# One half of the array's partitions for each head of a cross attention, and a new order of steps

## What is computed

```python
x = x + _L0_attn_ref(_layernorm(x, axis=-1), L0_attn_gamma)
x = x + _L0_xattn_ref(_layernorm(x, axis=-1), ctx_1024, ctx_1024, ...)
x = x + _L0_ffn_ref(_layernorm(x, axis=-1), ...)
```

```python
scores = jnp.einsum('bhqd,bhkd->bhqk', q, k) / jnp.sqrt(jnp.float32(dk))
scores = scores + slopes[None, :, None, None] * dist[None, None, :, :]
attn = jax.nn.softmax(scores, axis=-1)
```

## Time and profile before

| | |
|---|---|
| median of 3 runs | 316.39 us (316.10 to 316.88) |
| profiled execution, its span | 312.0 us (no other time of it is recorded) |
| busy: PE, DVE, ACT, POOL | 232.0, 177.7, 105.6, 73.2 us |
| L766 DVE reduces, x88 | 49.9 us |
| L606 ACT exponentials, x80 | 44.7 us |
| L959 PE maxima matmuls, x172 | 33.5 us |
| L980 PE score matmuls, x64 | 28.2 us |
| mean granted PE clock | 0.830 |

### The profile page before, as it was taken

How to read it: one execution, slowest core, us unless ns; L and a number is a source line. 1 busy time by engine, 2 the same in 40 slices (tenths; PEclk the granted TensorE clock), 3 DMA queues, 4 the chain that set the end, 5 groups by cost and what they waited for, 6 DMA issues and landing times.

```text
span 312.0 us, 3052 instructions
## 1 busy us (share of the span) xinstructions
PE 232.0 (74%) x993; PEld 99.4 (32%) x993; DVE 177.7 (57%) x433; ACT 105.6 (34%) x182; POOL 73.2 (23%) x122
## 2 busy tenths in 40 slices
PE   0876756587889688978998996997985599843184
PEld 0332522122323233443533344242443133223031
DVE  3148639598563678868539797672866260133160
ACT  1333332301484545245164703622611522610000
POOL 7118420001630008117100310640001080001080
PEclk9997876855959889965999998599997569995569
DMA  3790007711003400213340101436200210000221
GB/s 76 230 224 2 3 0 183 161 47 32 13 3 113 90 0 2 61 33 117 122 81 0 36 3 41 137 101 137 65 0 6 66 78 0 0 1 2 81 88 34
DMA packets 26409, 19.25 MB, mean 62 GB/s; under 512 B 12249, under 2 KB 25025, under 8 KB 26305
## 3 DMA queue, kind: packets, MB, share of 16 engines
q1 hardware_dynamic: 26393, 19.05, 23.5%
HBM read 13.64 MB, written 5.41 MB: 61 GB/s over the span
## 4 chain that ended last, share of the span: by engine, by line
PE 45%; DVE 24%; DMA 9%; ACT 8%; issue 5%; SPq 4%; POOL 3%; ACTq 0%; DVEq 0%; POOLq 0%
PE bank L1044 10%; DVE nm L766 9%; PE bank L858 5%; PE bank L1002 4%; PE bank L959 4%; SPq L306 4%; PE bank L1000 4%; PE bank L980 3%; DMA xs<-in_x_dram 3%; ACT pt L606 3%; PE bank L933 2%; DVE y L659 2%; POOL w L499 2%; PE bank L1030 2%; PE bank L901 2%
## 5 line engine op out<-in xcount | busy, mean ns | idle before, releaser
L766 DVE TENSOR_REDUCE nm<-bank 128x3 f32<-128x462 f32 x88 | 49.9, 617 | 18.2 <-PE bank L959 17.0
L606 ACT ACTIVATE pt<-bank 128x512 f32<-128x512 f32 x80 | 44.7, 597 | 26.0 <-PE bank L980 18.4
L959 PE MATMUL bank<-kA,qs 128*128 128x308 bf16 (+1 forms) x172 | 33.5, 298 | 14.1 <-DVE nm L766 7.9
L1044 PE MATMUL bank<-ym,ewT 128*128 128x512 f32 x64 | 32.4, 664 | 6.2 <-DVE ym L837 6.2
L499 POOL TENSOR_TENSOR w<-w,ab 128x512 f32<-128x512 f32 x8 | 11.9, 1506 | 99.2 <-ACT ab L530 99.2
L520 POOL TENSOR_TENSOR ym<-mask_all,y3T 128x512 f32<-128x512 bf16 x16 | 25.5, 1623 | 33.3 <-DMA mask_all<-e_scratch 33.3
L980 PE MATMUL bank<-qs,kB 128*128 128x512 bf16 x64 | 28.2, 501 | 3.4 <-ACT pt L606 2.7
L837 DVE TENSOR_TENSOR ym<-mask_all,y3T 128x512 f32<-128x512 bf16 x16 | 21.6, 1407 | 16.0 <-DMA mask_all<-e_scratch 16.0
L901 PE MATMUL bank<-y1Tg,y1T 128*128 128x512 f32 x32 | 20.8, 738 | 5.5 <-ACT w L544 3.2
L676 DVE TENSOR_REDUCE rm<-bank 128x1 f32<-128x512 f32 x16 | 11.0, 690 | 24.2 <-PE bank L902 24.2
L959 PEld LDWEIGHTS bank<-kA,qs 128*128 128x128 bf16 x172 | 12.7, 102 | 37.8 <-DVE nm L766 26.0
(11 more groups left out here) (155 smaller groups left out, 307.2 us busy)
## 6 DMA issues: line engine op xcount, KB each, us to landing
mask_all<-e_scratch SPq DMA_DIRECT2D x8, 512.0 KB, 4.7
qs<-q_scratch SPq DMA_DIRECT2D x8, 384.0 KB, 5.1
q_scratch<-qpart SPq DMA_DIRECT2D x4, 384.0 KB, 2.5
...
```

The costliest lines, as they stand in the source:

```text
L606: nc.scalar.activation(pt[:, n % PT_RING, :], ST[n % 2][:, :], ACT.Exp).then_inc(exps, 1)
L766: v.tensor_reduce(negated[:, GROUP * g:GROUP * g + heads], MX[n % 2][:, 0:heads * J].rearrange("p (s j) -> p s j", s=heads), AX.X, ALU.max ...
L959: last = mm(MX[n % 2][:, at * J:(at + heads) * J], qs[:, b % 2, a, tile(t)], kA[:, s:s + heads, a, 0:J], start=True, stop=True)
L1044: last = mm(YV[:, :], ewT[:, e, :], ym[:, e, :], start=False, stop=(e == E - 1))
```

## The change

Each head has 48 + 3 + 3 rows in one half of the partitions, 0 to 53 or 64 to 117: `place(h)` gives pair and half, heads of odd groups of four the upper one. The weights' rows are reordered on input to match (`head_rows`). There is one key stack `ks` with two buffers by batch, no zero blocks, and `kA` and `kB` go; their loads (8 + 8 of 120 KB) become 8. A part of `maxima` is three pairs for both banks: lower halves write MX[0] and upper halves MX[1], in turn, each matmul with 154 columns; both banks wait for the part before. The number and size of DVE's reduces stay. `scores` goes through the halves in turn with its two banks. The maxima are loaded into `qs` by two DMAs, not one. The orders of all engines are new; of these the diff shows the parts up to the first maxima of batch 1 or 2.

```diff
-AUG = 2 * ROWS
+AUG = ROWS
 MAXROW = AUG + 3
+USED = MAXROW + 3
+
+
+def place(h):
+    g, k = h // R, h % R
+    return g // 2 * R + k, g % 2
...
     "sync": """
-        query:0 keys:0 more_keys:0 stats1:1 mT:0 query:1 stats1:2 divide:0.0 mT:1 mask:0 query:2 divide:1.0
-        stats1:3 mT:2 mask:1 query:3 store:0 store:1 divide:2.0 mT:3 mask:2 mask:3 store:2 store:3
+        keys:0 query:0 more_keys:0 mT:0 stats1:1 query:1 mT:1 mask:0 stats1:2 query:2 stats1:3 mT:2 mask:1
+        query:3 store:0 mT:3 mask:2 mask:3 store:1 store:2 store:3
     """,
     "gpsimd": """
-        rstd1:0 sub:0 rstd1:1 weights:0 rstd2:0 sub:1 rstd1:2 rstd2:1 sub:2 rstd1:3 rstd3:0 rstd2:2 select:0
+        rstd1:0 sub:0 weights:0 rstd1:1 rstd2:0 sub:1 rstd2:1 rstd1:2 rstd1:3 sub:2 rstd3:0 rstd2:2 select:0
...
     "scalar": """
-        y1T:0 dist:0 ab:0 sub:0 self:0 weights:0 y2T:0 keys:0 query:0 y1T:1 dist:1 ab:1 sub:1 mT:0 self:1
-        scores:0.0 scores:0.1 scores:0.2 scores:0.3 scores:0.4 scores:0.5 y2T:1 query:1 y1T:2 values:0.1 dist:2
+        y1T:0 dist:0 ab:0 sub:0 self:0 weights:0 keys:0 y2T:0 query:0 y1T:1 dist:1 ab:1 sub:1 self:1 mT:0 y2T:1
+        scores:0.0 query:1 scores:0.1 scores:0.2 scores:0.3 y1T:2 scores:0.4 scores:0.5 dist:2 scores:0.6
+        values:0.1 scores:0.7 scores:0.8 scores:0.9 scores:0.10 scores:0.11 ab:2 values:0.3 aoT:0 sub:2 y3T:0
...
     "vector": """
-        stats1:0 y1:0 dist:0 rowmax:0 stats1:1 sub:0 weights:0 self:0 gather:0 y1:1 y2:0 query:0 keys:0 dist:1
-        rowmax:1 maxima:0.0 maxima:0.1 maxima:0.2 maxima:0.3 maxima:0.4 maxima:0.5 maxima:0.6 maxima:0.7
-        maxima:0.8 maxima:0.9 maxima:0.10 mcat:0 sub:1 stats1:2 self:1 y1:2 gather:1 stats1:3 y2:1 query:1
-        dist:2 maxima:1.0 maxima:1.1 rowmax:2 maxima:1.2 maxima:1.3 maxima:1.4 maxima:1.5 maxima:1.6 sub:2
+        stats1:0 y1:0 dist:0 rowmax:0 sub:0 weights:0 stats1:1 self:0 gather:0 y1:1 y2:0 keys:0 query:0 dist:1
+        rowmax:1 stats1:2 sub:1 maxima:0.0 maxima:0.1 maxima:0.2 self:1 maxima:0.3 maxima:0.4 maxima:0.5
+        maxima:0.6 maxima:0.7 maxima:0.8 maxima:0.9 maxima:0.10 mcat:0 gather:1 y2:1 y1:2 stats1:3 query:1
+        dist:2 maxima:1.0 rowmax:2 maxima:1.1 maxima:1.2 maxima:1.3 divide:0.0 maxima:1.4 sub:2 maxima:1.5
+        maxima:1.6 divide:0.1 maxima:1.7 maxima:1.8 wo:0 maxima:1.9 y3:0 self:2 maxima:1.10 mcat:1 route:0
...
     "tensor": """
-        y1T:0 dist:0 weights:0 ab:0 self:0 gather:0 keys:0 y2T:0 query:0 y1T:1 dist:1 maxima:0.0 maxima:0.1
-        maxima:0.2 maxima:0.3 maxima:0.4 maxima:0.5 maxima:0.6 maxima:0.7 maxima:0.8 maxima:0.9 maxima:0.10 ab:1
-        mT:0 self:1 gather:1 scores:0.0 scores:0.1 scores:0.2 scores:0.3 scores:0.4 scores:0.5 y2T:1 scores:0.6
-        query:1 values:0.0 y1T:2 values:0.1 dist:2 maxima:1.0 maxima:1.1 scores:0.7 divide:0.0 maxima:1.2
-        scores:0.8 ab:2 scores:0.9 maxima:1.3 maxima:1.4 maxima:1.5 scores:0.10 maxima:1.6 scores:0.11
-        values:0.2 maxima:1.7 values:0.3 divide:0.1 maxima:1.8 aoT:0 maxima:1.9 wo:0 maxima:1.10 self:2 y3T:0
-        mT:1 route:0 gather:2 mask:0 scores:1.0 scores:1.1 scores:1.2 scores:1.3 y2T:2 query:2 scores:1.4
-        experts:0 y1T:3 scores:1.5 values:1.0 scores:1.6 dist:3 maxima:2.0 values:1.1 maxima:2.1 scores:1.7
+        y1T:0 dist:0 ab:0 weights:0 self:0 gather:0 keys:0 y2T:0 query:0 y1T:1 dist:1 ab:1 self:1 maxima:0.0
+        maxima:0.1 maxima:0.2 maxima:0.3 maxima:0.4 gather:1 maxima:0.5 maxima:0.6 maxima:0.7 maxima:0.8
+        maxima:0.9 maxima:0.10 mT:0 y2T:1 scores:0.0 query:1 scores:0.1 y1T:2 scores:0.2 scores:0.3 values:0.0
+        scores:0.4 scores:0.5 dist:2 scores:0.6 maxima:1.0 values:0.1 maxima:1.1 scores:0.7 scores:0.8
+        maxima:1.2 scores:0.9 ab:2 maxima:1.3 scores:0.10 divide:0.0 scores:0.11 maxima:1.4 values:0.2
+        maxima:1.5 values:0.3 maxima:1.6 divide:0.1 maxima:1.7 aoT:0 maxima:1.8 wo:0 maxima:1.9 self:2 y3T:0
+        maxima:1.10 route:0 mT:1 gather:2 mask:0 scores:1.0 scores:1.1 y2T:2 scores:1.2 query:2 scores:1.3
+        experts:0 y1T:3 scores:1.4 values:1.0 scores:1.5 dist:3 scores:1.6 maxima:2.0 values:1.1 maxima:2.1
...
-        kA = sb("kA", [P, 2, PAIRS, JP], BF16)
-        kB = sb("kB", [P, 2, PAIRS, JP], BF16)
+        ks = sb("ks", [P, 2, PAIRS, JP], BF16)
...
-        nm = sb("nm", [P, T, H])
+        nm = sb("nm", [P, 2, T, PAIRS])
...
-        a_ps, maxed, mcat_ready, mT_ps, mT_sb = sem("a_ps"), sem("maxed"), sem("mcat_ready"), sem("mT_ps"), sem("mT_sb")
+        a_ps, maxed = [sem(f"a_ps{s}") for s in range(2)], [sem(f"maxed{s}") for s in range(2)]
+        mcat_ready, mT_ps, mT_sb = sem("mcat_ready"), sem("mT_ps"), sem("mT_sb")
...
-        GROUPS = -(-T * H // GROUP)
-        MAX_GROUPS = [range(g, min(g + 2, GROUPS)) for g in range(0, GROUPS, 2)]
+        GROUPS = -(-T * PAIRS // GROUP)
...
-            load(kA[:, :, :, :], k_aug[0], kaug_in)
-            load(kB[:, :, :, :], k_aug[1], kaug_in)
-            for par in range(2):
-                load(qs[AUG:P, par, :, :], q_aug, qaug_in)
+            for s in range(2):
+                load(ks[s * HALF + AUG:s * HALF + USED, :, :, :], k_aug[s], kaug_in)
+            for s in range(2):
+                load(qs[s * HALF + AUG:s * HALF + MAXROW, :, :, :], q_aug, qaug_in)
...
-            def stack_keys(stacks, b, s_in):
+            def stack_keys(b):
 
                 for s in range(2):
-                    load(stacks[s * ROWS:(s + 1) * ROWS, s, :, :],
-                         k_scratch[b].rearrange("(a s c) k j -> s (c k) a j", s=2, c=DK)[s], s_in)
+                    load(ks[s * HALF:s * HALF + ROWS, b % 2, :, :],
+                         k_scratch[b].rearrange("(a s c) k j -> s (c k) a j", s=2, c=DK)[s], ks_in)
 
             def stats1(b, _):
-                if b >= 1:
-                    sp.wait_ge(k_out, 3 * B * ONE)
-                    sp.wait_ge(maxed, b * GROUPS)
-                    stack_keys(kA, b, kA_in)
+                sp.wait_ge(k_out, 3 * B * ONE)
+                if b >= 2:
+                    sp.wait_ge(st_ps, (b - 1) * R * ITEMS)
+                stack_keys(b)
 
             def keys(b, _):
                 sp.wait_ge(k_ready, 1)
                 write_keys(0)
                 sp.wait_ge(k_out, 3 * ONE)
                 sp.wait_ge(kaug_in, 2 * ONE)
-                stack_keys(kA, 0, kA_in)
-                stack_keys(kB, 0, kB_in)
+                stack_keys(0)
...
-                    load(qs[s * ROWS:(s + 1) * ROWS, b % 2, :, :],
+                    load(qs[s * HALF:s * HALF + ROWS, b % 2, :, :],
                          q_scratch.rearrange("(a s c) k n -> s (c k) a n", s=2, c=DK)[s], qs_in)
-
-            def divide(b, f):
-                if f == 0 and b + 1 < B:
-                    sp.wait_ge(st_ps, (b + 1) * R * ITEMS)
-                    stack_keys(kB, b + 1, kB_in)
 
             def mT_(b, _):
                 sp.wait_ge(mT_sb, b + 1)
                 load(m_scratch.rearrange("r (a n) -> (r a) n", n=S), mT[:, :], m_out)
                 sp.wait_ge(m_out, ONE * (b + 1))
-                load(qs[MAXROW:MAXROW + 6, b % 2, :, :].rearrange("p a n -> p (a n)"), m_scratch, m_in)
+                for s in range(2):
+                    load(qs[s * HALF + MAXROW:s * HALF + USED, b % 2, :, :].rearrange("p a n -> p (a n)"),
+                         m_scratch.rearrange("(i s) w -> s i w", s=2)[s], m_in)
...
             def maxima(b, k):
-                negated = nm[:, :, :].rearrange("p t h -> p (t h)")
-                for g in MAX_GROUPS[k]:
-                    n, heads = b * GROUPS + g, min(GROUP, T * H - GROUP * g)
-                    dve.wait_ge(a_ps, n + 1)
-                    v.tensor_reduce(negated[:, GROUP * g:GROUP * g + heads],
-                                    MX[n % 2][:, 0:heads * J].rearrange("p (s j) -> p s j", s=heads),
-                                    AX.X, ALU.max, negate=True).then_inc(maxed, 1)
+                pairs = slice(GROUP * k, min(GROUP * (k + 1), T * PAIRS))
+                heads = pairs.stop - pairs.start
+                for s in range(2):
+                    dve.wait_ge(a_ps[s], b * GROUPS + k + 1)
+                    v.tensor_reduce(nm[:, s, :, :].rearrange("p t a -> p (t a)")[:, pairs],
+                                    MX[s][:, 0:heads * J].rearrange("p (s j) -> p s j", s=heads),
+                                    AX.X, ALU.max, negate=True).then_inc(maxed[s], 1)
...
             def maxima(b, k):
                 if k == 0:
-                    pe.wait_ge(kA_in, 2 * ONE * (b + 1))
+                    pe.wait_ge(ks_in, 2 * ONE * (b + 1))
                     pe.wait_ge(qs_in, 2 * ONE * (b + 1))
                     if b == 0:
                         pe.wait_ge(setup_sb, 8)
                     if b >= 1:
                         pe.wait_ge(mT_sb, b)
-                for g in MAX_GROUPS[k]:
-                    n = b * GROUPS + g
-                    if n >= 2:
-                        pe.wait_ge(maxed, n - 1)
-                    at = 0
```

(57 more changed lines are left out.)

61 lines of the change are left out of this document (28 added, 33 removed).

## The result

The changed kernel takes 336.93 us (336.67 to 337.21), the kernel before 316.25 beside it: a ratio of 1.0653 [1.0598, 1.0707]. The direction was forecast, the size was not: +20.7 us for +5.9, and outside the range.

What follows compares the result with a forecast made beforehand. No engine is full: PE and DVE alternating banks bound the bare stage, both nearly full in mixed stages. Terms +2.0 +2.75 +0.5 -1.5 +2.8 -0.6 = +5.95 us gave 322.3 us from 316.4; own range 319 to 326, whole range 311 to 329.

Steps and rivals of the forecast that it cites:

- Part 1: Batch 0's bare maxima stage: fills wait for the second bank; a step 1.75 us for 1.30, the stage 19.5 for 14.5.
- rival B: Maxima steps: the halves don't run beside each other, so a pair costs 308 columns; 329 us, chance 0.13.
- Parts 2 and 3: New order around batch 0's bare stage, then exponentials moved behind it: y2T:1 2.0 us later, maxima:1.0 4.75 us late.
- +2.05, -1.4 and -1.0: Batch 1: values:0.1 paid (+2.05), routing, gather and y2T:2 earlier (1.4), experts:0 no longer behind scores:1.4 (1.0).
- Part 4: Mixed stages of batches 1 to 3: PE's column savings against shape switches and DVE's bare steps, together +0.5 us a stage.
- +0.5, -1.5 and +2.8 us: Changes in lateness over batches 1, 2 and 3: maxima:2.0 5.3 late, maxima:3.0 3.8 late, y3T:2 6.6 late.
- Rival A: Mixed stages: switches cost nothing and PE's savings pay, about 3.3 us a stage; 311 us, chance 0.22.
- D: Batch 0's late stage delays the query stack's DMA, dist:2 stays at half clock: +4, 326 us; counted in forecast's range (0.50).

## Why the prediction was wrong

*Part 1, right.* Halves overlap (rival B falls), the fill is blocked, step and stage have the forecast length. Alone it costs 1.7%, 5.4 us.

*Parts 2 and 3, too early from the start.* `self:1` ended at 69.2 (forecast 67.1), since `diag` came at 59.76 and not 57.9. How late each step starts against the kernel before, in us:

| | forecast | measured |
|---|---|---|
| y2T:1 | 2.0 | 4.1 (95.82) |
| maxima:1.0 | 4.75 | 8.3 (114.31) |
| maxima:2.0 | 5.3 | 10.1 (173.31) |
| maxima:3.0 | 3.8 | 12.6 (228.98) |
| y3T:2 | 6.6 | 19.2 (257.11) |
| end of the span | 6.0 | 22.9 |

Of the 4.1 us at y2T:1 the old layout in the new order has 1.2; the rest comes with the blocked stage. Behind y2T:1 the clock was at its half level, as the window shows; from y2T:1 to dist:2 it was 0.57, where that stretch had 0.86, and dist:2 began at 108.80 and not at 105.1:

```profile
97.00:106.00 9.00, 8.36 (x29) 2.60 (x28) 3.71 (x14) 7.03 (x13) 2.84 (x9) 0.50 0.28 91
```

The order itself was priced too high: alone it makes maxima:1.0 3.0 us late and maxima:3.0 0.1, and costs 0.2% [-0.4, +0.7]. (A small slip of the sum: in batch 1 the +2.05, -1.4 and -1.0 make -0.35, and I left it out.)

*Part 4, wrong, and the step that failed.* Its +0.5 us a stage priced columns, switches and bare steps, all with durations of the stages before, at 0.93 to 1.00 of the clock: that the change might move their clock was put at nothing, without a reason. The batches whose stages I had at +0.5, -1.5 and +2.8 us (from `maxima:1.0` to y3T:2) took 1.8, 2.5 and 6.6 us longer, and the tail behind, forecast at -0.6, 3.7. In the place of the +0.5 the runs showed stages at 0.88, 0.88 and 0.70 of the clock, half rows that cost 2.6 to 3.1% beside a blocked fill, and 1.7 to 2.8 us that come back between the second mark and the last when PE is given idle work. The Trainium skill ("TensorEngine Tiling (Array Packing)", Key Properties) had a switch of tiling mode drain the engine. The rows bear it out as a small term: from L995's start to the half-row step behind it is 1.06 us (below), from L1003's to a full-row step 0.96 (182.18 to 183.14 above). But half rows in the maxima, which put two such switches around each step, cost 0.0% [-0.7, +0.7] with the blocked fill.

```profile
115.60 1.12 PE L995 MATMUL bank<-pt,vt 128*128 128x512 f32 x2
116.66 0.37 PE L952 MATMUL bank<-ks,qs 51*128 51x154 bf16 x6
```

*Rival A, PE's relief, fell.* PE was relieved, 24.6 us of maxima matmuls for 33.5, and its clock went down: half rows in the maxima alone took it from 1.00 to 0.88 and from 0.92 to 0.75 in two stages. *D*, worse order, was the only place where the forecast spoke of the clock, in one stage and for 4 us; at that place it came about.

What the runs settle: order 0.2%; blocked fill 1.7 to 2.2%; half rows beside it 2.6 to 3.1%, of which the trace shows equal matmuls at half clock. Added work brings the clock back in the mixed stages, and in one kernel of three 1.7% of the time. What they don't: the 1.1% that full rows bank by bank (1.0125) keep over the old layout in the same order (1.0017; the intervals overlap), how much of the half rows' cost is anything but clock, and which of the two tails an execution gets.
